# GpSimd instead of VectorE scales the source rows of the third layer's gathered features

## What is computed

```python
edge_index = jnp.stack([src, dst])
x = _layernorm(x + _L0_gnn_ref(x, edge_weight, edge_attr_3, edge_index, ...), axis=-1)
x = _layernorm(x + _L1_gnn_ref(x, edge_index), axis=-1)
x = _layernorm(x + _L2_gnn_ref(x, edge_index, edge_attr_32, ...), axis=-1)
x = _layernorm(x + _L3_gnn_ref(x, edge_attr3_2x32, src, dst, ...), axis=-1)

# layer 2: an MLP per edge, and the maximum per destination
e_feat = jnp.concatenate([x[rol], x[col], edge_attr], axis=-1)
v = jax.nn.relu(e_feat @ W1 + b1) @ W2 + b2
x_cand = jax.ops.segment_max(v, col, num_segments=num_nodes)
return jnp.maximum(x_cand, x[:, -v.shape[-1]:])

# layer 3: attention
feat_src = (feat @ W2s + b2s).reshape(n, H, F)
feat_dst = (feat @ W2d + b2d).reshape(n, H, F)
en, ev = feat_src[src], feat_dst[dst]
```

## Time and profile before

| | us |
|---|---|
| median of three runs | 1801.41 |
| lowest and highest of them | 1792.41, 1803.49 |
| the profiled execution | 1790.27 |
| its span, first to last instruction | 1788.5 |
| VectorE busy in it | 1317.8 (74%) |
| GpSimd busy in it | 1284.0 (72%) |

### The profile page before, as it was taken

The page is one execution under the profiler, slowest core; times in us unless marked ns, Lnnn a source line. Parts: engine busy times, 40 slices in busy tenths (PEclk is TensorE's granted clock), DMA queues, the critical chain, the costliest instruction groups (busy, mean ns, idle before and its releaser), DMA issues.

```text
span 1788.5 us, 14348 instructions
## 1 busy us (share of the span) xinstructions
PE 730.4 (41%) x3676; PEld 542.7 (30%) x3676; DVE 1317.8 (74%) x2358; ACT 483.9 (27%) x1063; POOL 1284.0 (72%) x1839
## 2 busy tenths in 40 slices
PE   6920554444125205605336000546505777661500
PEld 3310222221012105504336000445404777651400
DVE  9953799898399998775756798388765988986400
ACT  7923211111001014413334211324302334442100
POOL 8877788888788825857888558880068847888776
PEclk9965778688568657957678555668756666765655
DMA  8159211111111022412222430000001111110000
GB/s 322 52 164 372 82 30 27 24 32 27 16 19 29 11 91 84 141 46 79 103 91 84 168 142 5 5 16 21 31 22 23 32 28 34 33 30 10 10 11 10
DMA packets 61789, 114.23 MB, mean 64 GB/s; under 512 B 25309, under 2 KB 46344, under 8 KB 60920
## 3 DMA queue, kind: packets, MB, share of 16 engines
q1 hardware_dynamic: 24432, 80.96, 12.4%
q0 software_dynamic: 31296, 12.76, 5.0%
q10 hardware_dynamic: 5960, 19.43, 2.9%
HBM read 60.87 MB, written 55.21 MB: 65 GB/s over the span
## 4 chain that ended last, share of the span: by engine, by line
POOL 55%; DVE 24%; issue 16%; PE 3%; DMA 1%; ACT 1%; another core or an unknown queue 0%; POOLq 0%; DVEq 0%; SPq 0%; ACTq 0%
POOL joined L774 12%; POOL out L917 11%; POOL A_msg L859 7%; POOL gtmp L764 6%; POOL edge_sums L865 5%; POOL A_dst L774 5%; POOL work L774 5%; DVE work L1519 4%; DVE A_dst L1519 3%; DVE stat L1530 2%; POOL out_short L774 2%; POOL A_msg L774 2%; DVE work L1530 1%; DVE A_msg L2306 1%; DVE joined L1618 1%
## 5 line engine op out<-in xcount | busy, mean ns | idle before, releaser
L764 POOL MEMSET gtmp<- 64x64 f32 x830 | 138.9, 167 | 206.8 <-DMA table<-A_dst 128.7
L1345 PE MATMUL bank<-w2fold,work 128*128 128x384 f32 x392 | 185.4, 617 | 201.8 <-DVE work L1519 180.5
L917 POOL DMA_INDIRECT out<-A_dst,out_i x196 | 216.4, 1104 | 59.9 <-POOL gtmp L764 34.0
L774 POOL DMA_INDIRECT A_dst<-in_x,dst_i x196 | 214.2, 1093 | 58.2 <-issue 34.5
L1530 DVE TENSOR_REDUCE work<-work 128x80 f32<-128x1280 f32 (+3 forms) x147 | 204.8, 1423 | 65.7 <-ACT work L1051 33.9
L774 POOL DMA_INDIRECT joined<-x_pos,A_tmp x168 | 174.0, 1036 | 48.9 <-POOL gtmp L764 34.1
L1345 PEld LDWEIGHTS bank<-w2fold,work 128*128 128x128 f32 x392 | 87.0, 239 | 299.0 <-issue 258.2
L1519 DVE TENSOR_TENSOR work<-bank,work 128x384 f32<-128x384 f32 (+1 forms) x294 | 154.0, 593 | 4.4 <-remote 3.6
L1012 ACT ACTIVATE work<-A_tmp,b1col,w1col 65x256 f32<-65x256 f32 x98 | 58.8, 600 | 356.6 <-PE bank L1345 309.4
L1383 PE MATMUL bank<-nodes_w,small 128*128 128x128 f32 (+1 forms) x784 | 118.0, 307 | 69.3 <-ACT small L1041 50.1
L774 POOL DMA_INDIRECT work<-table,pos_i x88 | 120.9, 1374 | 24.1 <-POOL gtmp L764 20.3
(11 more groups left out here) (394 smaller groups left out, 2164.1 us busy)
## 6 DMA issues: line engine op xcount, KB each, us to landing
work<-in_x SPq DMA_DIRECT2D x26, 960.0 KB
x_pos<-joined SPq DMA_DIRECT2D x13, 990.0 KB
out<-work ACTq DMA_DIRECT2D x13, 960.0 KB
A_tmp<-ew_turned_rows ACTq DMA_DIRECT2D x49, 130.0 KB
table<-A_dst SPq DMA_DIRECT2D x2, 3136.0 KB
edge_sums<-A_dst SPq DMA_DIRECT2D x2, 3136.0 KB
table<-A_dst SPq DMA_DIRECT2D x13, 448.0 KB
A_tmp<-in_edge_attr_2x SPq DMA_DIRECT2D x49, 112.0 KB
```

The lines of the kernel that those rows point to most:

```text
L764: pool.memset(tile, 0.0).then_inc(cleared, 1)
L774: pool.indirect_dma_start(out=column(t), out_offset=None, in_=of, in_offset=bass.IndirectOffsetOnAxis(ap=idx[:, t:t + 1], axis=0), bounds_ ...
L917: pool.indirect_dma_start(out=out, out_offset=bass.IndirectOffsetOnAxis(ap=out_i[:, t:t + 1], axis=0), in_=A_dst[:, t, :], in_offset=None, ...
L1345: last = nc.tensor.matmul(banks[2 * (u % PAIRS_DEEP) + j][:, 0:PATHS], hid_rows[:, u % PAIRS_DEEP, j * P:(j + 1) * P], w2_rows[:], start=T ...
```

## The change

VectorE's seven `scale_sources` calls go away, in both branches. POOL gets them instead: a function of the same name is called once, behind POOL's 88th and last gather for layer 2 and ahead of its wait for `tables[4]`. It waits for the first window (`e_cat`) and, per chunk, for the same number of turns as before. A new semaphore `sources_scaled` counts the seven, and VectorE waits for all seven in front of the first step of each window of layer 3.

```diff
             for k, of, order in zip((3, 4), compact, WINDOW_ORDER):
 
+                if k == 4:
+                    scale_sources()
                 pool.wait_ge(table_stored, 16 * parts_until(k))
                 pool.wait_ge(gather_ok, k + 2)
...
+            def scale_sources():
+
+                pool.wait_ge(e_cat, 1)
+                for c in range(CHUNKS):
+                    pool.wait_ge(e_turned, SLOTS + min(END_QUADS + (c + 1) * CHUNK_QUADS, QUADS))
+                    pool.tensor_tensor(out=chunk(J_src, c), in0=chunk(J_src, c), in1=bcast(chunk(r3, c), FEAT),
+                                       op=ALU.mult).then_inc(sources_scaled, 1)
...
                 if k == 0:
+                    if layer == 1:
+                        v.wait_ge(sources_scaled, CHUNKS)
                     v.wait_ge(wide_in, layer + 1)
...
-            def scale_sources(c):
-                v.wait_ge(e_turned, SLOTS + min(END_QUADS + (c + 1) * CHUNK_QUADS, QUADS))
-                step(tt(chunk(J_src, c), chunk(J_src, c), bcast(chunk(r3, c), FEAT), ALU.mult))
...
                 for c in range(CHUNKS - 1):
-                    after.setdefault(7 * c + 9, []).append(partial(scale_sources, c))
                     after.setdefault(7 * c + 12, []).append(lambda c=c: center(c))
...
-                after.setdefault(QUADS - 1, []).append(partial(scale_sources, CHUNKS - 1))
```

More of the change, by code:

```diff
@@ L303, in gnn_kernel @@
         prod_used, node_seq, a_weighed = sem("prod_used"), sem("node_seq"), sem("a_weighed")
-        a_leaky = sem("a_leaky")
+        a_leaky, sources_scaled = sem("a_leaky"), sem("sources_scaled")
         final_ready, scattered = sem("final_ready"), sem("scattered")
@@ L2367, in _ @@
                 join_ends()
-                for c in range(CHUNKS):
-                    scale_sources(c)
                 seam(*maxima_seam, columns=slice(0, T))
```

## The result

The changed kernel takes 1812.55 us (median of 16 runs, 1795.05 to 1827.50); the kernel before took 1801.62 in 16 runs of the same session (1791.93 to 1807.00). The ratio is 1.0052, with a 95% interval of 1.0034 to 1.007: 9.4 us slower, 6.1 to 12.6. The forecast was 7.8 us slower and 1809. The profiled execution took 1806.48, against 1790.27 for the one of before. Those 16 us between two single executions turned out to be mostly chance (experiment e10), so I don't read them as the price.

A forecast was written before the change was run, and what follows sets the result against it. Between layer 2's last gather and the layer-3 table VectorE decides while POOL idles. Delays of 4.1 (first three scalings), 1.5 (fourth) and 2.1 (last), savings included, sum to 7.8 us: 1801.4 + 7.8 = 1809, range 1795 to 1820.

The forecast's parts named there:

- VectorE waits for POOL's product: Assumption that a VectorE operation with two SBUF inputs is held while POOL's scaling reads; without it the sum is -1.7 us.
- only POOL waits: Rival: POOL's operation never holds VectorE's, so only the saving of 1.7 us is left, 1799.7 us; chance 0.2.
- p: POOL's time for one scaling of 896 elements, taken as 2.1 us, with bounds of 1.5 and 2.9.
- the lower bound of 1.5: POOL's time for one scaling if the second read is free; the whole change would then be 4.8 us slower.
- 5p - 2.75: Sum of all places, p being POOL's time per scaling: 7.8 us slower at 2.1, 4.8 at 1.5, 11.8 at 2.9.
- c0: Chunk 0's scaling, on VectorE before window 2: removing it saves 0.6 of its 1.12 us, limited by the last gather's landing.
- c0 to c2 on POOL: First three scalings, run after layer 2's last gather: they delay VectorE's window 2 work, net 4.1 us late.
- 3p - 2.15: Net delay from the first three scalings at window 2, p being POOL's time for one: 4.1 us.
- c3: Chunk 3's scaling, after turn 30: holds the VectorE copy at 1230.46 that TensorE waits for, by 1.5 us.
- c4, c5: Scalings of chunks 4 and 5: each holds one VectorE operation, covered by idle time before the scans; cost nothing.
- The sign that I had named: Predicted evidence in the changed profile: the scans behind chunks 4 and 5 wait longer than 3.10 and 2.19 us.
- c6: Chunk 6's scaling, after turn 49: gets in behind VectorE's addition and delays the first product of `center` by 2.1 us.

The follow-up runs named there:

- e10: The kernel before, unedited, run and profiled again; ratio 0.9998 (0.998 to 1.0016) against the kernel before.
- e5: Changed kernel with each POOL scaling replaced by three memsets of 128x384 that write and don't read; ratio 0.9980 against the kernel before, stage 135.98 us.
- e2: Changed kernel with all seven scalings left out, POOL only waits and raises the semaphore; ratio 0.9986 against the kernel before, stage 136.02 us.
- e1: The changed kernel once more, unedited, for a second profile; ratio 1.0029 (0.9997 to 1.0061) against the kernel before, stage 144.08 us.
- e9: Kernel before plus one POOL product of 64x1 elements at the changed place, late in the program; ratio 0.9998 (0.9981 to 1.0015).
- e12: Kernel before with COPIES_FIRST (4, 9) for (4, 4), more ScalarE copies of x ahead of its first edge activation; 1792.84 us, ratio 0.9935.
- e11: Kernel before plus one POOL product of 64x1 elements ahead of POOL's first gather; ratio 1.0014 (0.9995 to 1.0034).
- e4: Kernel before with two of VectorE's scalings, chunks 0 and 2, moved later into VectorE's idle time; ratio 1.0000 (0.9974 to 1.0027), stage 136.08 us.
- e6: Changed kernel with three more POOL products of 128x256 on idle data behind each scaling; ratio 1.0030 against the kernel before, stage 144.12 us.

## Why the prediction came out right, and which steps did not

The time, 1812.55 for 1809, and the loss, 9.4 for 7.8, agree; the steps agree less well than the sum.

- **That VectorE waits for POOL's product.** Right, and it was the step that no row of before showed. e5 bears it out: same place, same busy time, no read, no loss. The rival "only POOL waits" is out, since the copy and the products have 1.0 to 4.0 us more than their length. The Trainium skill, SBUF — State Buffer, section Who interferes with whom, describes such a lock; the trace agrees for products, predicated copies and POOL products, with those numbers.
- **p, the price of a scaling.** Mis-sized: 1.66 to 1.70 us, not 2.1, near the lower bound of 1.5. Against the bound with a free second read that read cost about 0.2 us, not the 0.6 that one row's read rate gave. With p = 1.68 the formula 5p - 2.75 gives 5.65.
- **c0.** Wrong step: its saving was counted at 0.6, because window 2's last gather would still be under way. The gathers themselves ended 1.2 us earlier (42.37 for 43.58 after the start, e2), since the copy that held one of them for 2.30 came 1.12 sooner. The saving is 1.12 + 1.12 (e2: 2.27), not 1.7.
- **c0 to c2 on POOL.** Expected 3p - 2.15 with the three in one piece or alternating. They ran in one piece, and VectorE's product had been expected ahead of them. It stood behind them instead: 4.03 held (e1), 2.59 in the first profile, less 2.24 saved. That is 1.8 and 0.35, where the formula gives 2.9 at the measured p and gave 4.1.
- **c3.** Expected p - 0.6 = 1.5, measured 0.99 (3.12 for 2.13); at the measured p the formula gives 1.1. Right.
- **c4, c5.** Right that they cost nothing: a product each held by 1.1, and the scans behind them still waited 2.86 and 1.98. The sign that I had named, waits longer than 3.10 and 2.19, was wrong: the hold takes up the 1.12 that the removed scaling leaves.
- **c6.** Expected p = 2.1, measured 1.33. POOL's product waited for the addition to end, and VectorE's product then started 0.03 later and was held for what was left.
- **TensorE's clock.** A term that was not in the sum. Where it stayed low or fell, that cost 1.6 to 1.7 us at the next scan, more than c3 or c6. In the first profile of before TensorE went to the upper level (transposes of 0.39 us, 2.4 GHz) at the pause at 1190.33; in the changed kernel the same turn, behind the same pause of 0.38, still ran at the lower one (0.63 to 0.69, 1.2 GHz, a granted clock of 0.50), until about 1204:

```profile
1200.22 0.69 PE L1280 MATMUL bank<-ident,joined 128*128 128x128 f32 x2 [0.38 <-DVE joined L2313]
...
1203.15 0.63 PE L1280 MATMUL bank<-ident,joined 128*128 128x128 f32 x2
...
1205.01 0.39 PE L1280 MATMUL bank<-ident,joined 128*128 128x128 f32 x2
```

That is about 1.7 us at the scan behind it (31.20 after the stage's start; before 30.67, less the 1.12 of c0; e2 29.46). Most of it didn't lengthen the stage: VectorE's product with std came 1.7 later, into the same piece of POOL's, and was held for 1.4 less than in e1. e1 and e2 have the changed order of VectorE there without that delay, so the change doesn't bring it every time. In e1 the clock fell again for 3.5 us, at 1261.97, after TensorE had been idle for 2.06 behind the held copy of c3 (0.92 in the first profile of before), and the next scan was 1.6 later than the held copy explains. In the first profile of the change TensorE was idle for 1.51 there, and the clock stayed up. e10 has 1.2 us of this kind, in an unchanged kernel: behind a pause of 5.74 the transposes of 0.63 go on there from 1278.39 to 1283.21, over two turns of 2.9 and 1.9, and in the first profile of before, behind one of 5.72, over one.

The stage then adds up. For e1: 138.29 - 2.27 + 4.03 + 0.99 + 1.33 = 142.4, and the 1.6 of the clock at the fourth scan makes 144.0, for 144.08 measured. For the first profile: 138.29 - 2.27 + 2.59 + 0.99 + 1.33 = 140.9; with the 1.7 of the clock, less 0.3 by which the fifth and sixth scans came sooner than in e2, that is 142.3.

**What the sum doesn't hold.** The stage explains 4.0 and 5.8 us of a loss measured as 9.4 (6.1 to 12.6) and, the second time, 5.2 (-0.5 to 11.0). The two measurements of the same kernel agree with each other and with 6 us. That the sum came closer to the first is luck in part: p was too high by 0.4 five times over, and the clock was left out. One thing stays open. Of the 58 executions of the five kernels with POOL's scalings 23 took 1816 to 1828 us, while all those of the kernel before and of e2 to e5 and e9 to e12 stayed below 1815; that may be the rest of the 9.4. The one such execution that was profiled, e1's, had lost its extra time before 225 us (its first gather from `x_pos` starts at 222.8), with VectorE idle between its small operations as in e10 and for longer. How a product at 1217 us could bear on that isn't shown, and I know of no step that leads there; a tiny product (e9, e11) doesn't bring it, and whether the longer ones do by their length wasn't tried.

## What to carry to other kernels

Before moving an elementwise operation from VectorE to an idle POOL, look at what VectorE executes beside it: with products or predicated copies there, POOL's products come back as VectorE's waiting, and several POOL products issued back to back can all be paid for by one VectorE operation beside them. First find the one or two instances that are on the path and try a place in the same engine's idle time; e4 had the whole gain that way. And when two profiles differ mostly far away from the edit, profile the kernel before once more, and ask what in the queue there can be put in front of the thing that waits.

## What the runs showed of the hardware that I had not expected

- Three POOL products of 1.66 us each ran in one piece of 5.00 with a VectorE product waiting 4.03 us beside them (e1). Yet with a short POOL product of another tile behind the first scaling, VectorE got in between the two (held 0.74, e6), though nothing made POOL wait there.
- POOL memsets of the same length (1.37 to 1.39 for three of 128x384) held nothing (e5).
- A second SBUF input costs POOL little: 1.66 to 1.70 us for 896 products per partition, about 1.77 ns each over the 0.09 fixed of the earlier trace rows, where reading one input and writing took 1.54.
- In some executions VectorE idles for 5 and 7 us around the same few small operations, beside an unbroken row of POOL's gathers, where in others of the same kernel it goes straight on (e10 and the first profile of before). Through ScalarE's queue this moved the start of the stage by some 11 us.
